# fc1_U of the third token block ahead of the last two token tiles of the output projection

## The reference

```
h    = x + ctx @ out_U @ out_V + out_b            # output projection and residual
x2   = layernorm(h)
hmid = gelu(x2 @ fc1_U @ fc1_V + fc1_b)           # 1024 -> 512 -> 4096
h    = h + hmid @ fc2_U @ fc2_V + fc2_b           # 4096 -> 512 -> 1024
```

## Time and profile before

| | |
|---|---|
| median of 3 runs | 1074.34 us (1073.59 to 1078.11) |
| the profiled execution: its own time | 1080.18 us |
| span of its slowest core, core 6 | 1078.6 us |
| spans of the eight cores | 1064.2 to 1078.6 us |
| PE busy on core 6 | 997.8 us, 93% of the span |
| DVE, ACT, POOL busy | 539.1, 535.1, 189.1 us |

### The profile page before, as it was taken

The page is one execution under the profiler, slowest core; times in us unless marked ns, Lnnn a source line. Parts: engine busy times, 40 slices in busy tenths (PEclk is TensorE's granted clock), DMA queues, the critical chain, the costliest instruction groups (busy, mean ns, idle before and its releaser), DMA issues.

```text
span 1078.6 us, 17097 instructions; the slowest of 8 cores (1064.2 to 1078.6 us)
## 1 busy us (share of the span) xinstructions
PE 997.8 (93%) x6217; PEld 463.7 (43%) x6278; DVE 539.1 (50%) x1016; ACT 535.1 (50%) x646; POOL 189.1 (18%) x185
## 2 busy tenths in 40 slices
PE   2999999798799899799898999999999999999998
PEld 1444444374344444344333444444444444444443
DVE  6568989555355355555458980012030424734523
ACT  2335254145688688778886454333323354241321
POOL 2021422501000001200022137850000000033030
PEclk9999999899899999989999999999999999999999
DMA  8983389595123325963467999950210025041211
GB/s 167 208 215 76 82 148 184 89 167 72 49 52 61 48 47 75 169 89 62 64 192 213 121 145 163 210 103 6 57 23 0 2 40 113 5 118 78 40 78 78
DMA packets 128927, 105.41 MB, mean 98 GB/s; under 512 B 102608, under 2 KB 109904, under 8 KB 127568
## 3 DMA queue, kind: packets, MB, share of 16 engines
q0 software_dynamic: 19536, 53.85, 27.4%
q1 hardware_dynamic: 109312, 50.46, 21.6%
HBM read 94.16 MB, written 16.78 MB: 103 GB/s over the span
## 4 chain that ended last, share of the span: by engine, by line
PE 62%; DVE 15%; issue 8%; ACT 6%; DMA 6%; SPq 3%; POOL 0%; DVEq 0%; ACTq 0%; POOLq 0%
PE db L1482 10%; PE db L1448 10%; PE db L365 7%; PE ub L923 6%; PE db L391 6%; PE sd L1068 5%; PE db L379 4%; ACT AT L1078 4%; PE ct L1103 3%; DVE st L430 3%; PE ub L933 3%; PE db L1461 3%; DMA QS<-ST 2%; PE db L1435 2%; PE db L1420 2%
## 5 line engine op out<-in xcount | busy, mean ns | idle before, releaser
L1078 ACT ACTIVATE AT<-sd 128x1024 bf16<-128x1024 f32 (+1 forms) x320 | 265.7, 896 | 88.2 <-PE sd L1068 85.4
L1531 ACT ACTIVATE HM<-db,csts 128x512 bf16<-128x512 f32 x128 | 81.0, 685 | 140.5 <-PE db L1448 140.4
L1068 PE MATMUL sd<-QS 64*128 64x512 bf16 (+3 forms) x640 | 102.6, 356 | 28.0 <-ACT AT L1078 17.4
L1482 PE MATMUL db<-HM,f2U 128*128 128x512 bf16 x500 | 120.7, 383 | 2.0 <-ACT HM L1531 1.3
L1448 PE MATMUL db<-P,f1V 128*128 128x512 bf16 x504 | 120.5, 381 | 1.5 <-ACT P L1519 1.0
L923 PE MATMUL ub<-WQK,x1T 128*64 128x392 bf16 x1024 | 101.9, 335 | 1.6 <-DVE tta L419 1.6
L1103 PE MATMUL ct<-AT,VA 128*64 128x512 bf16 (+3 forms) x640 | 87.9, 354 | 1.4 <-DVE AT L1085 1.4
L1482 PEld LDWEIGHTS db<-HM,f2U 128*128 128x128 bf16 x512 | 50.3, 98 | 63.3 <-issue 7.6
L1448 PEld LDWEIGHTS db<-P,f1V 128*128 128x128 bf16 x512 | 50.2, 98 | 62.4 <-issue 4.5
L1625 DVE CAST P<-db 128x1024 bf16<-128x1024 f32 x4 | 4.9, 1225 | 140.4 <-PE db L1482 140.4
L1068 PEld LDWEIGHTS sd<-QS 64*128 64x128 bf16 x640 | 29.7, 93 | 104.4 <-issue 99.3
(11 more groups left out here) (162 smaller groups left out, 1290.8 us busy)
## 6 DMA issues: line engine op xcount, KB each, us to landing
S<-xs POOLq DMA_DIRECT2D x32, 512.0 KB, 11.5
xs<-X SPq DMA_DIRECT2D x4, 2048.0 KB, 7.7
x_out<-S SPq DMA_DIRECT2D x15, 512.0 KB, 2.7
wr<-wrT POOLq DMA_DIRECT2D x4, 1024.0 KB, 17.6
X<-x_in SPq DMA_DIRECT2D x2, 2048.0 KB, 14.9
f1V<-fc1V POOLq DMA_DIRECT2D x16, 256.0 KB, 5.1
f2U<-fc2U POOLq DMA_DIRECT2D x32, 128.0 KB, 5.1
WQK<-kU POOLq DMA_DIRECT2D x4, 784.0 KB, 11.3
```

What stands on the lines that cost most here:

```text
L1068: m = pe.matmul(SD[q % 2][:, TB * s + off:TB * (s + 1)], QS[64 * s:64 * s + 64, T * (2 * SET[p] + 1) + 128 * i:T * (2 * SET[p] + 1) + 128 ...
L1078: act.activation(c3(AT[q % 4])[:, :, off:TB], c3(SD[q % 2])[:, :, off:TB], AF.Exp, scale=0.125)._wait_ge(a_qk, q + 1).then_inc(a_exp, 1)
L1482: m = pe.matmul(DB[2 + p2 // 2][:, TB * (p2 % 2):TB * (p2 % 2 + 1)], f2U[ic // 8][:, 512 * (ic % 8) + 128 * p2:512 * (ic % 8) + 128 * (p2 ...
L1531: m = act.activation(HM[i % 4][:, TB * e:TB * (e + 1)], DB[job_db[("H", b, i)]][:, TB * e:TB * (e + 1)], AF.Gelu_apprx_tanh, bias=scol("fc ...
```

## The change

In PE's order, the two F jobs of block 2 move from behind OP 15 to between OP 13 and OP 14. Since banks are given by position, F 2 now takes double banks 2 and 3, and OP 14 and OP 15 take 0 and 1, where the first two H jobs will go. ACT's third border moves from behind tile 15 to behind tile 13. On DVE the reciprocals of tile 13 now follow `dve_op(13)` at once, and those of tile 14 stand behind `dve_op(15)`, together with those of tile 15. The lists of SP and POOL are unchanged. The work itself is unchanged.

```diff
     first_jobs = ([("OP", t) for t in range(8)] + [("F", 0, 0), ("F", 0, 1)]
                   + [("OP", t) for t in range(8, 12)] + [("F", 1, 0), ("F", 1, 1)]
-                  + [("OP", t) for t in range(12, 16)] + [("F", 2, 0), ("F", 2, 1)])
+                  + [("OP", 12), ("OP", 13), ("F", 2, 0), ("F", 2, 1), ("OP", 14), ("OP", 15)])
+
+    borders = (7, 11, 13)
...
     def act_phase2(act):
         act_op_sd(act, 0)
         for t in range(NT):
-
-            border = t in (7, 11, 15)
-            if not border:
+            if t not in borders and t + 1 < NT:
                 act_op_sd(act, t + 1)
             act_zu(act, t, (o_nm, t + 1), t, rsC, nmC)
-            if border:
-                act_p1(act, t // 4 - 1)
-                if t + 1 < NT:
-                    act_op_sd(act, t + 1)
+            if t in borders:
+                act_p1(act, borders.index(t))
+                act_op_sd(act, t + 1)
...
     def dve_phase2(dve):
         for t in range(NT):
             dve_op(dve, t)
-            if t and t not in (8, 12):
+            if t and t - 1 not in borders:
                 dve_op_rs(dve, t - 1)
-            if t in (7, 11, 15):
+            if t in borders or t == NT - 1:
                 dve_op_rs(dve, t)
```

## The result

The changed kernel takes 1085.82 us (median of 6 runs; five lie between 1082.99 and 1088.09, and the sixth, 1187.11, is a slow execution, in which the four cores of one die show a granted clock of 0.88) against 1075.46 us for the kernel before (6 runs): a ratio of 1.008, 95% interval 1.0058 to 1.0101. A second comparison gave 1.0102 (1.0066 to 1.0138). It is slower, as forecast, but by 9 to 11 us instead of 6.5, and beyond the end of the range, 1083.7.

The account below looks back on a forecast made before the run. PE, busy 93% of the span, was taken to bound the kernel. Bare tail 3.83, wait before F 0.75 and clock 1.9 summed to +6.5 us, 1080.8 us against the median; range 1077.4 to 1083.7.

Parts of the forecast that it names:

- the second chain: Before the first A: ACT's normalizations of tiles 14 and 15, F's evacuation, table load, gelu; within 0.1 us of PE's own.
- Part 1: Before H 0: it waits for OP 14's evacuation instead of F's, so PE's own chain gains 1.05 us.
- Part 3: Behind OP 15: only OP 15 and two H cover tile 15's chain, so the first A starts 3.83 us later.
- The table load: Before the first gelu: 1.28 us by the trace; by the Trainium skill's 2.66 us the loss would be some 1.4 larger.
- Part 4: Behind the new idle stretch of about 5 us at the first A: PE's granted clock falls, costing 1.9 us.
- Rival A: Gap before the first A without clock loss: the clock holds at 2.4 GHz; +4.6 us, 1078.9; chance 0.15.
- Part 5: POOL's last fc2_U load moves from 650.17 to about 656.5, hidden; bias additions begin 6 us later, PE about as much.
- Part 2: Before F of block 2: 24 matmuls instead of 48 cover the transposes of tiles 8 to 11; wait 0.75 us.
- Rival C: Slower still: the last core has the largest transpose wait, 2.55, and clock loss, 3.0; +9.4 us, 1083.7; chance 0.10.
- The base: Whole kernel: the median time before the change, to which +6.5 us was added to give 1080.8 us.
- Slower: Whole kernel: the outcome of a time over 0.5% longer, starting at 1079.7 us; chance 0.60.

Follow-up runs that it names:

- The first experiment: Changed kernel with the first two gelus on ACT ahead of the normalizations of tiles 14 and 15; ratio to the kernel before 1.0022 (0.9978 to 1.0065).

## Why the prediction was right or wrong

**Bound and direction: right.** PE sets the time, a PE late at the first A stays late, and the removed 1.05 us was worth nothing because the second chain (normalize, load, gelu) became the longer one.

**Part 1, the wait removed: right.** There is no wait before H 0.

**Part 3, the bare tail: right in size.** Forecast 3.83 us; 3.8 by the stage, and 3.8 where the other wait was taken out. From DVE's addition to the first A I had 8.19 us, and it is 8.16. The gap shows as 4.88 instead of 5.1 because I set the end of the two H 0.2 us early, by the start of a next matmul and not by the shown end of the last. The first experiment shows that the chain is ACT's.

**The table load: the trace was right.** The load took 1.28 us and the gelu began 0.02 us behind it, here as before. The drain that the Trainium skill adds to it ("ScalarE: Activation LUTs", "What ACT_TABLE_LOAD costs") would have made the chain 1.4 us longer, as an estimate from its figure of about 1380 ns, and is not in this trace.

**Part 4, the clock: right,** 1.9 us in the mean, on every core. That the clock falls is shown to come from idle time alone (8 of 8 cores in the old order too, with 1.7 us lost). Rival A, that it holds, falls at this length of gap.

**Part 5, POOL: right.** The last load of fc2_U was forecast some 6 us later. On core 3 it began 28.3 us behind OP 12, where it had been 20.9 to 23.5 us on the eight cores before, and the time behind the first A is as it was.

**Part 2, the wait before F: mechanism right, size wrong.** I took 0.75 us. F was late by 1.7 us in the first profile, and by 1.5 over twelve cores: this term is mis-sized by 0.75 us or more. The landings that I read off were right for that one execution; from eight draws between 0 and 2.55 I took the median where the mean, 1.0, was at hand. Its cause, which the prediction did not name, is the fc2_U load beside the transposes.

**From the sum to the time: the step that failed.** I added the sum of one core's terms to the time of the kernel. With the terms as measured that sum is 7.2 us and describes the median core, which moved by 7.0. The metric is the slowest of eight, and it moved by 10.4 in the mean of nine runs, or by 9.3 without the one run that probably owes its length to something else. Part of this would be expected, as the new terms differ from core to core. But drawing each core's extra time at random from those measured, on top of the spans of before, gives only some 7.5 us. So 2 to 3 us of the slowest core's shift are not explained by the terms as I measured them: the tenth percentile of the spans moved by 6.6 us, the ninetieth by 9.6 (8.8 without that run). With F's wait taken out (the load behind the transposes) the slowest core stood 6.7 us over that of before in its own comparison, near its terms of 3.8 + 2.2; that points to the wait before F, but on six runs only. A long wait before F that also lowers the clock, as once seen above with 3.39 us, would act in that direction; no trace of the changed kernel shows one. The cause stays open. Rival C had the size for another reason (the worst wait and the worst clock on one core) and ended at 1083.7, still 2 us short.

**The base.** My 1080.8 started from 1074.34, the median of three runs. Later medians of the same kernel were 1075.46 to 1077.96. That is 1.1 us or more of the 5.0 us by which the forecast was missed.

**The chances.** Slower had 0.60. With the wait before F at its mean and the base at its later value it should have stood higher; the part that put the result outside the range was not in the sum at all.

## What to carry to other kernels

When a job is moved from behind a chain of evacuation, statistics and activation to ahead of it, ask what covered that chain: the wait it removed was 1 us, the cover it took away 3.8 us, and the idle time that opened cost another 1.9 us of clock. Before moving the job, look for an idle engine that can take its evacuation: here DVE did, and the same wait vanished with nothing moved. And where the metric is the slowest of eight cores, a sum of one core's terms forecasts the median core: here that one moved by the sum, 7 us, and the slowest by 9 to 10.

## What the runs showed of the hardware that was not expected

A 1 MB load of plain rows delays transposing DMAs beside it. From issue to landing they took 4.1 to 10.1 us in the profile of the changed kernel with the load under way, and 3.0 to 3.3 us on all eight cores when the load waited for them.

Whether the clock falls at an idle stretch of 2.6 to 2.8 us is not a matter of its length alone. With 2.58 us it fell on 4 of 8 cores in one kernel and on 7 of 8 in its near twin, which differ only in the time of a load; with 2.75 us in the old order, on 1 of 8. What decides it there is open. Before the first A it fell on none of eight cores at 1.8 us and on 40 of 40 at 4.15 us and more. Elsewhere it fell behind less, too: near 180 us of the kernel before, PE stood idle for 1.93 us on all eight cores, and on core 2 alone the clock fell behind it, to a mean of 0.79 over 8 us.
